# Causal attention and a dense mixture of experts: maxima by pairs of heads, three score banks, expert outputs weighed in one pass and added by POOL

## The reference, cut to what matters

```python
def _gqa(x, wq, wk, wv, wo):             # 16 heads of 8 channels, 4 key/value heads
    ...
    attn = jnp.einsum('bqhd,bkhd->bhqk', q, k) * scale
    attn = jnp.where(causal, attn, -jnp.inf)
    attn = jax.nn.softmax(attn, axis=-1)
    out = jnp.einsum('bhqk,bkhd->bqhd', attn, v).reshape(B, S, C)
    return out @ wo.T

def _moe(x, gate_w, expert_w):           # 8 experts, the best 2 weigh
    ...
    for e in range(N_EXPERTS):
        out = out + comb[:, e, None] * (t @ expert_w[e].T)
    return out.reshape(B, S, C)

h = x + _gqa(_rmsnorm(x, attn_norm_w), wq, wk, wv, wo)
out = h + _moe(_rmsnorm(h, ffn_norm_w), gate_w, expert_w)
```

## Time and profile before

| what | value |
|---|---|
| three runs | 1682.2, 1681.0, 1675.95 us; median 1681.0 |
| the profiled execution's own time | 1679.97 us |
| its span, first to last instruction | 1678.4 us |
| mean granted clock of PE, share of full speed | 0.869 |
| first blocks, up to the first piece | 887.7 us |
| 96 pieces of unit 0, guard and its DMAs | 887.7 to 946.8 us |
| the 192 steps | 946.8 to 1626 us |
| what is left of `post_h` | 1626 to 1678.4 us |

### The profile page before, as it was taken

How to read it: one execution, slowest core, us unless ns; L and a number is a source line. 1 busy time by engine, 2 the same in 40 slices (tenths; PEclk the granted TensorE clock), 3 DMA queues, 4 the chain that set the end, 5 groups by cost and what they waited for, 6 DMA issues and landing times.

```text
span 1678.4 us, 19240 instructions
## 1 busy us (share of the span) xinstructions
PE 1266.5 (75%) x6144; PEld 578.6 (34%) x6144; DVE 1185.9 (71%) x2767; ACT 719.3 (43%) x1560; POOL 515.5 (31%) x650
## 2 busy tenths in 40 slices
PE   3513988788888677565759687988899889988783
PEld 1201445454444323232323232433333333333232
DVE  4889747555555599998969685868876887688234
ACT  2434672144444410122130266546465546644751
POOL 4414770022111258767660122112111202120211
PEclk9755997999999878787765699989999999999996
DMA  3000100000000000011115201112020202000010
GB/s 96 0 0 1 47 23 1 26 1 1 0 1 0 1 10 0 1 31 21 42 24 81 30 1 28 29 17 31 2 32 7 41 1 33 4 1 1 3 39 12
DMA packets 23441, 30.14 MB, mean 18 GB/s; under 512 B 2927, under 2 KB 16111, under 8 KB 23055
## 3 DMA queue, kind: packets, MB, share of 16 engines
q1 hardware_dynamic: 20750, 26.99, 8.6%
q10 hardware_dynamic: 2592, 1.93, 0.4%
HBM read 22.50 MB, written 6.42 MB: 17 GB/s over the span
## 4 chain that ended last, share of the span: by engine, by line
PE 41%; DVE 34%; POOL 9%; ACT 8%; issue 7%; DMA 1%; ACTq 0%; DVEq 0%; POOLq 0%
PE PS L583 8%; PE PS L566 7%; DVE SS L1090 6%; PE PS L540 5%; DVE XA L1169 5%; PE PS L361 3%; DVE RB L1007 3%; PE PS L364 3%; DVE RB L1008 3%; ACT RB L1457 3%; DVE st L671 3%; POOL rs L1524 2%; PE PS L377 2%; PE PS L254 2%; PE PS L626 2%
## 5 line engine op out<-in xcount | busy, mean ns | idle before, releaser
L1457 ACT ACTIVATE RB<-PS 128x512 f32<-128x512 f32 (+3 forms) x768 | 340.3, 494 | 312.6 <-PE PS L566 308.3
L1090 DVE TENSOR_REDUCE SS<-PS 128x1 f32<-128x512 f32 (+3 forms) x768 | 374.5, 548 | 73.8 <-PE PS L543 61.9
L540 PE MATMUL PS<-B 96*128 96x512 bf16 (+3 forms) x768 | 259.3, 355 | 48.8 <-DVE XA L1169 20.7
L566 PE MATMUL PS<-B 96*128 96x512 bf16 (+3 forms) x768 | 241.7, 339 | 39.9 <-ACT RB L1457 34.7
L1658 POOL TENSOR_SCALAR_AFFINE_SELECT RB<-RB 128x512 f32<-128x512 f32 x128 | 81.3, 635 | 526.8 <-ACT RB L1457 526.6
L583 PE MATMUL PS<-RB,B 128*32 128x512 f32 (+3 forms) x1536 | 172.7, 522 | 7.6 <-ACT RB L1464 7.3
L1522 POOL TENSOR_SCALAR rs<-mv 128x4 f32<-128x4 f32 (+1 forms) x68 | 23.4, 345 | 419.0 <-DVE mv L675 417.4
L566 PEld LDWEIGHTS PS<-B 96*128 96x128 bf16 x768 | 73.2, 100 | 164.7 <-ACT RB L1457 130.8
L540 PEld LDWEIGHTS PS<-B 96*128 96x128 bf16 x768 | 77.1, 101 | 152.4 <-DVE SS L1090 87.5
L445 PE MATMUL PS<-RB,w_hspread 128*128 128x512 f32 x128 | 82.8, 784 | 61.0 <-POOL RB L1622 51.2
L935 DVE TENSOR_TENSOR RB<-RB,PS 128x512 f32<-128x512 f32 x64 | 43.8, 685 | 106.7 <-ACT RB L1336 60.5
(11 more groups left out here) (231 smaller groups left out, 2033.6 us busy)
## 6 DMA issues: line engine op xcount, KB each, us to landing
B<-scrQ SPq DMA_DIRECT2D x72, 128.0 KB
scrQ<-B SPq DMA_DIRECT2D x6, 384.0 KB, 2.6
B<-scrK SPq DMA_DIRECT2D x36, 64.0 KB
X<-in_x SPq DMA_DIRECT2D x8, 256.0 KB, 8.5
out_dram<-X SPq DMA_DIRECT2D x8, 256.0 KB, 4.1
B<-in_w SPq DMA_DIRECT2D x3, 576.0 KB, 4.7
B<-in_zeros SPq DMA_DIRECT2D x9, 128.0 KB
B<-in_rope SPq DMA_DIRECT2D x1, 1024.0 KB, 4.8
```

The source lines that it names most:

```text
L540: ins = pe.matmul(p[:, 0:w], qs[u % 3][:, h, 128 * i:128 * i + 128], keys_of(u, h)[:, 512 * c:512 * c + w], start=True, stop=not diagonal)
L566: pe.matmul(p[:, 0:w], keys_of(u, 4 * kl + z)[:, 128 * kt:128 * kt + 128], qs[u % 3][:, 4 * kl + z, 512 * qc + off:512 * qc + 512], start= ...
L1090: dve.tensor_reduce(MX[:, u % 2, i, h, c:c + 1], bank(bank_of["first", u, n])[:, 0:first_width(i, c)], AX, ALU.max).then_inc(s["mx1"], 1)
L1457: act.activation(RB[:, 4 * (step % 3) + z, 0:w], bank(bank_of["score", step, z])[:, 0:w], ACT.Exp).then_inc(s["ex2"], 1)
```

## The change

1. **Maxima by pairs of heads.** `PAIRS` takes the place of `FIRST`: PE writes the same piece for heads h and h + 1 into two neighbouring banks, and one `tensor_reduce` takes both, with two maxima as its result: 48 pairs per unit in place of 96 pieces. PE's matmuls are the same.
2. **Banks.** Scores go round banks 0, 1, 2 in all steps; pairs go round (3, 4) and (5, 6); the product has bank 7. The heads, the guard and the slices of `post_h` and of the late pass take a place in the pair ring, or in the score ring (slices 0 and 6).
3. **Spread by content.** `AHEAD` gives each step as many pairs as its share of the exponentials (weights by width, in `held`): 3 or 2 in a 512-wide step, 1 in a narrow one. A unit's pairs begin right behind those of the unit before and end at step 16 of the unit before it is used (18 for unit 1). The guard of unit u is at step 17 (19).
4. **Order.** DVE reduces one pair (or none, where two or more places of the pair ring were taken at the end of the step before), then does the slices of the *previous* step, then reduces the rest; the guard follows the last pair. ACT and POOL, too, do the slices of a step one step later, ACT between exponentials 1 and 2.
5. **Experts.** For 128 tokens PE writes all 8 experts' outputs into one pair of banks; one DVE `tensor_tensor` multiplies the 1024 columns by the weights, spread over each expert's 128 columns, into an SBUF buffer (`SHARE`, two of them, in the free tiles HN and WX). POOL adds 512 + 512, 256 + 256, 128 + 128 columns, and the last 128 to XA. DVE waits for POOL (`xs_h`) before it writes a buffer again and before the statistics (now slice 14). `post_h` has 18 slices.

```diff
-        FIRST = [(h, i, c) for h in range(8) for i in range(8) for c in range(i // 4 + 1)]
+        PAIRS = [(h, i, c) for h in range(0, 8, 2) for i in range(8) for c in range(i // 4 + 1)]
...
+            held.append(held[-1] + {512: 1920, 384: 1490, 256: 1030, 128: 760}[second_span(n, kt)[1]])
+        AHEAD = {}
+        since, GUARD_AT = 0, {}
+        for u in range(1, 8):
+            until = held[24 * (u - 1) + (19 if u == 1 else 17)]
+            for j in range(48):
+                at = next(t for t in range(192) if held[t + 1] >= since + (until - since) * (j + 1) / 48)
+                AHEAD.setdefault(at, []).append((u, j))
+            since, GUARD_AT[at + 1] = until, u
...
-        POST_SLICES = 17
+        POST_SLICES = 18
...
+        SHARE = [HN[:, :, :].rearrange("p a t -> p (a t)"), WX[:, :]]
...
-            def next_1(step):
-                ring_1[0] += 1
-                return 2 + ring_1[0] % 4 if step < 168 else ring_1[0] % 6
...
+            def next_score():
+                score_ring[0] += 1
+                return score_ring[0] % 3
+
+            def next_pair():
+                pair_ring[0] += 1
+                return 3 + 2 * (pair_ring[0] % 2)
...
+            def first_1(u, n):
+                h, i, c = PAIRS[n]
+                k = next_pair()
                 w = first_width(i, c)
                 diagonal = c == i // 4
...
+                for a in range(2):
+                    p = room(k + a)
+                    ins = pe.matmul(p[:, 0:w], qs[u % 3][:, h + a, 128 * i:128 * i + 128],
+                                    keys_of(u, h)[:, 512 * c:512 * c + w], start=True, stop=not diagonal)
+                    if diagonal:
+                        ins = pe.matmul(p[:, w - 128:w], identb[:, :], msk[:, 0, :], start=False, stop=True)
+                    banks.lend(k + a, s["mx1"], 48 * u + n + 1)
...
-                k = (4 * step + z) % 2 if step < 168 else next_1(step)
+                k = next_score()
...
-                ahead = [n for n in range(5 * r, min(5 * r + 5, 96))] if u < 7 else []
+                ahead = AHEAD.get(step, [])
                 for z in range(4):
-                    for n in ahead[z:z + 1]:
-                        first_1(step, u + 1, n)
+                    for v, n in ahead[z * len(ahead) // 4:(z + 1) * len(ahead) // 4]:
+                        if n == 0:
+                            ready_1(v)
+                        first_1(v, n)
...
             def highest(u, n):
-                h, i, c = FIRST[n]
-                dve.wait_ge(s["mm1"], 96 * u + n + 1)
-                dve.tensor_reduce(MX[:, u % 2, i, h, c:c + 1], bank(bank_of["first", u, n])[:, 0:first_width(i, c)],
-                                  AX, ALU.max).then_inc(s["mx1"], 1)
+                h, i, c = PAIRS[n]
+                w = first_width(i, c)
+                p = bank(bank_of["first", u, n], 2).rearrange("p (a t) -> p a t", a=2)
+                dve.wait_ge(s["mm1"], 48 * u + n + 1)
+                dve.tensor_reduce(MX[:, u % 2, i, h:h + 2, c], p[:, :, 0:w], AX, ALU.max).then_inc(s["mx1"], 1)
...
-                    for half in range(2):
-                        dve.wait_ge(s["mo_h"], 8 * g + 2 * j + half + 1)
-                        for q in range(4):
-                            ins = dve.scalar_tensor_tensor(XA[:, 4 * g + j, :], quarter(bank(bank_of["post", g, k, half]), q),
-                                                           comb[:, j, 4 * half + q:4 * half + q + 1], XA[:, 4 * g + j, :],
-                                                           ALU.mult, ALU.add)
...
+                    p = bank(bank_of["post", g, k], 2).rearrange("p (e c) -> p e c", e=8)
+                    dve.wait_ge(s["mo_h"], 4 * g + j + 1)
+                    if 4 * g + j >= 2:
+                        dve.wait_ge(s["xs_h"], 4 * g + j - 1)
+                    dve.tensor_tensor(SHARE[j % 2].rearrange("p (e c) -> p e c", e=8), p,
+                                      comb[:, j, :].unsqueeze(2).to_broadcast([128, 8, 128]), ALU.mult).then_inc(s["mx_h"], 1)
-                if k == 13:
+                if k == 14:
+                    dve.wait_ge(s["xs_h"], 4 * g + 4)
                     stats(g, xa_tile, "i")
...
+            for step in range(LAST_STEPS + 1):
+                ahead = AHEAD.get(step, [])
+                early = 1 if lent_last.get(step - 1, 0) < 2 else 0
+                for u, n in ahead[:early]:
+                    highest(u, n)
+                    if n == 47:
+                        guard(u)
+                if step:
+                    slices(step - 1)
+                for u, n in ahead[early:]:
...
+                if 10 <= k < 14:
+                    j = k - 10
+                    z = SHARE[j % 2]
+                    pool.wait_ge(s["mx_h"], 4 * g + j + 1)
+                    for w in (512, 256, 128):
+                        own.done(pool.tensor_tensor(z[:, 0:w], z[:, 0:w], z[:, w:2 * w], ALU.add))
+                        own.wait()
+                    pool.tensor_tensor(XA[:, 4 * g + j, :], XA[:, 4 * g + j, :], z[:, 0:128], ALU.add).then_inc(s["xs_h"], 1)
```

More of the change, by code:

```diff
@@ L54 @@
 mm1 mx1 nm1 gt1 mf1 sm1 gd1 sc2 ex2 mk2 pv2 os2 ot2 at2
[L55 removed]
+tp_h y_h po_h xo_h th_h hb_h lg_h lc_h lx_h ee_h mo_h mx_h xs_h
 """.split()
@@ L635, in tensor_program @@
             ready_1(0)
-            for n in range(96):
-                first_1(0, 0, n)
+            for n in range(48):
+                first_1(0, n)
             guard_1(0)
@@ L1191, in vector_program, with slices @@
+            def slices(step):
+                if 0 <= step - PLAG - 1 < 192:
+                    n, kt = STEPS[step - PLAG - 1]
                     if kt == 4 * GROUPS[n][2] + 3:
                         divide(n)
-                for n in ahead[2:]:
-                    highest(u + 1, n)
-                if u < 7 and r == 19:
-                    guard(u + 1)
-                if u < 7 and r == 20:
-                    guard_row(u + 1)
+                if step in GUARD_AT:
+                    guard_row(GUARD_AT[step])
@@ L1202, in vector_program @@
                     post_h(g, k)
+            for n in range(48):
+                highest(0, n)
+            guard(0)
+            guard_row(0)
+            for step in range(LAST_STEPS + 1):
[8 more added lines that the diff above has]
+                for u, n in ahead[early:]:
+                    highest(u, n)
+                    if n == 47:
+                        guard(u)
         def scalar_program():
@@ L1463, in sums @@
                     act.wait_ge(s["ot2"], n - 1)
-                act.activation(row(12 + n % 2), bank(6), ACT.Copy).then_inc(s["os2"], 1)
+                act.activation(row(12 + n % 2), bank(7), ACT.Copy).then_inc(s["os2"], 1)
             def post_h(g, k):
@@ L1496, in scalar_program @@
             act.wait_ge(s["nm_c"], 36)
-            for step in range(LAST_STEPS):
+            for step in range(LAST_STEPS + 1):
                 if step < 192:
```

126 lines of the change are left out of this document (59 added, 67 removed).

## The result

The kernel after the change takes 1768.03 us (median of four runs, 1767.02 to 1769.46), the kernel before 1678.47 beside it (four runs, 1674.99 to 1682.2): a ratio of 1.0534, 95% interval 1.0505 to 1.0563. Forecast were 1631, range 1588 to 1670. The profiled execution, one of the four, has a span of 1767.3 us against 1678.4.

| stretch, us | before | after |
|---|---|---|
| first maxima, first reduction to last | 44.7 | 53.7 |
| from there to the first exponential | 13.3 | 8.9 |
| the steps | 680.0 | 756.8 |
| tail | 51.6 | 55.8 |

The account below looks back on a forecast made before the run. No engine was full; PE, nearest to it, and ACT were taken to wait for each other in turn. Terms 0 - 30 - 10 + 1 - 27 + 18 - 2 = -50 us took the median 1681 to 1631 us, range 1588 to 1670.

Parts of the forecast that it names:

- 6 us late, three times: Statistics of chunks g = 0, 2, 4 wait for POOL's sums behind selects in diagonal steps: +18 us, bounds 0 and +36.
- The third: Rival: POOL's sums, waiting for selects in a loop, become the bound in the steps: slower, 1701 us, chance 0.08.
- The floor: In the steps: 679.2 us less 142 of PE's waits leaves about 537 us of work PE keeps.
- Pairs: Maxima by pairs save DVE 25 us over all, mostly off the path: 0, bounds -3 and +3.
- The named sign, PE's waits for reductions above 35 us: Sign that would show the forecast wrong: whole pairs make PE wait over 35 us for reductions.
- the forecast 0 (bounds -3 and +3): Prologue: pairs could gain or lose 3 us at half clock, and an earlier guard would wait longer for the DMA queue.
- Three banks, -30: In the steps: PE three scores ahead cuts its 80 us of waiting for ACT: -30 us, bounds 0 and -80.
- +1 for unit 7: Unit 7: its scores have three banks in place of six: +1 us, bounds 0 to +4.
- Spread, -10: In the steps: pieces following ACT's share take 10 of 35 us of PE's waits for maxima, bounds -30 and +10.
- Experts, -27 and +18: In the steps: PE's waits for experts' sums on DVE go, -27 us; POOL's late sums add +18.
- Tail, -2: Tail: reciprocal earlier by 3.7 us, last chunk 1.1 longer: -2 us taken, bounds -6 and +2.
- ACT idle as long as before: Sign that would show the forecast wrong: ACT's idle time does not fall.

Follow-up runs that it names:

- e1: Kernel before with the experts' part alone: products on DVE in single banks, sums on POOL, statistics one slice later; 1661.43 us, ratio 0.989.
- e8: Kernel after with slices back at the end of their own step on DVE, ACT and POOL, and DVE's division ahead of the pairs; 1663.31 us, ratio 0.9882.
- e5: e1 with pieces also spread by content: single pieces in four banks, guard at step 17, two score banks; 1642.84 us, ratio 0.9786.
- e7: Kernel after with single pieces in four places, slices back in their own step on all three engines, division ahead of the pieces; 1625.28 us, ratio 0.9669.
- g1: Kernel before with only the slices moved a step later on DVE, ACT and POOL, no experts' sums on POOL; 1776.65 us, ratio 1.0584.
- g3: e7 with two score banks in place of three, and five places for the rest; 1657.53 us, ratio 0.9875.
- g2: e7 with the first sum of 512 columns on DVE for the two chunks in the tail only; 1618.39 us, ratio 0.9629.
- f4: e7 with the first sum of 512 columns on DVE in all chunks; 1627.75 us, ratio 0.9703.
- e3: Kernel before with three score banks and three single piece banks in place of two and four, up to step 168; 1690.30 us, ratio 1.0072.

## Why the prediction was wrong

The sign, by one step: **the order of the slices**. The prediction spoke of moved slices only where it came to POOL's select, as 6 us late, three times, and gave the move itself no term in the sum. It measured 58.0 us on e1, 93.7 on the kernel before, 105.7 on the kernel after (half of it DVE's, 49.6). With it undone (e8) the kernel takes 1663.31 us, in the range, though that is 15 us under the kernel before where 50 were forecast: the pairs took the rest. The parts, each added to the one above it:

| added | steps, us | median, us |
|---|---|---|
| experts (before to e1) | -20.5 | -17.0 |
| spread (e1 to e5) | -18.3 | -18.6 |
| third score bank, heads and guard in the ring, division first, pieces placed anew between the scores (e5 to e7) | -23.1 | -17.6 |
| pairs (e7 to e8) | +33.0 | +38.0 |
| order (e8 to after) | +105.7 | +104.7 |
| together | +76.8 | +89.6 |

The rows for it stood there: the earlier trace rows have PE waiting for both pieces and experts' sums, in one ring of banks, so the question was in which order DVE would take what PE had written, and the answer could be read from the code. None of the rivals had it either. The third made the right sign (1701) of another mechanism: in the kernel after POOL is 25% busy in the steps (190.9 of 756.8), DVE waits for it for 7.5 us there, and the same sums in e8 cost nothing of the kind.

**The floor**, 537 us that PE keeps because no matmul is dropped, was wrong too as a way to count: PE's busy time in the steps went from 556.5 us (e7) to 639.4 (g1) for the same work, where the forecast moved waits alone.

**Pairs**: taken as hidden, their blocking inside bounds of -30 to +10 on all waits for maxima. They cost 33.0 us in the steps with the order right (618.1 to 651.1), 35.1 on the kernel before, 20.1 under the wrong order. Of the 25 us that DVE was to save, the page shows 17.2 (374.5 to 357.3 busy), and they bought nothing, as DVE was not the fullest engine in any unit shown; the price was what comes with pairs, two places in place of four among it. In e8 DVE waits 85.8 us for PE ahead of a reduction, in e7 45.4, and PE waits 30.4 us with the array idle for reductions, in e7 21.2. The named sign, PE's waits for reductions above 35 us, gave no clear answer: 27.7 us with the array idle, 44.2 from the weight load. By the rule of the Trainium skill that was cited there (VectorE: DVE Perf Modes, "The TRN2 errata — SBUF-src ops pay a fixed extra latency per instruction") the saving would be 48 us, and it would have argued for the pairs still more; the busy time of the first maxima, added up form by form, fell from 50.9 to 45.0 us, 123 ns for each of 48 pairs, which agrees with the rule. With the overlap of one reduction and the next taken out it fell from 44.7 to 43.8.

In the prologue the forecast 0 (bounds -3 and +3) was +9.0 for the maxima and -4.4 for what follows, +4.6. At half clock (0.52) PE's filling of a pair and DVE's reducing overlap only in part; the prologue of the kernel after, waits:

```profile
PEld PS L569 <- DVE SS L1131: 30.8, 43, 1.3
PE PS L569 <- DVE SS L1131: 10.6, 22, 0.7
DVE SS L1131 <- PE PS L569: 6.4, 12, 0.8
DVE SS L1131 <- PE PS L572: 4.0, 13, 0.6
```

Both wait in turn; before, PE waited 24.1 us from the weight load and DVE never. The guard's first DMA, which had taken 5.63 us, took 1.53 as it began 9 us later, counted from the first reduction, after the loads: the DMA share is 0.54 from 935 to 940 us before, and 0.00 from 945 to 950 after. The prediction had that pairing of start and queue, with the sign turned.

**Three banks, -30, and +1 for unit 7**: -21 in units 0 to 6 (g3 to e7), +1.0 in unit 7 (56.1 to 57.1). Right in sign and too large, and right by another way than the one given, as PE did not stand still for less. **Spread, -10**: right in sign, -18.3. **Experts, -27 and +18**: -9 forecast together, -20.5 measured. Units 1 to 6, which hold the sums, gained 26.5 us, and units 0 and 7, which hold none before the last two steps, lost 6.0, at a granted clock of 0.85 and 0.86 in place of 0.89 and 0.91. In e1 DVE doesn't wait for POOL in the steps at all, so the 18 us of lateness did not come.

**Tail, -2**: it was +4.2. The reciprocal did come 1.35 us after the last heads, in place of 4.59, as forecast. What was missed is the ACT stream behind it. The timelines of the tail, kernel after:

```profile
1719.73 0.25 DVE L1171 RECIPROCAL SS<-PS 128x16 f32<-128x16 f32 x1
...
1727.85 1.65 ACT L1263 ACTIVATE RB<-XA,rs 128x128 f32<-128x128 f32 x4 [10.55 <-POOL rs L1572]
1729.40 0.57 ACT L1518 ACTIVATE SS<-PS 128x512 f32<-128x512 f32 x1
```

The copy of the heads (L1518) stands behind the normalisation of chunk g = 6, and that now waits for POOL's sums: 9.67 us from reciprocal to copy, where the kernel before took 3.80 (L1475 at 1642.42). That is +5.9; the last chunk, from the first of its matmuls to the statistics, went from 15.75 to 17.60, +1.9 where +1.1 was forecast; with the -3.2 it comes to +4.5. The rule that was cited against this part (the Trainium skill, GPSIMD Engine Reference, "4.1 Engine selection") held in the tail: g2's one sum on DVE in each slice gave 5.8 back. In the steps the same move brought nothing: f4 is 9.4 us slower than g2 by the median, 11.6 in the steps, a part of it in units without such a sum.

Of the signs named in advance: a reduction of 1024 columns near 1.2 us (1.22), the reciprocal (1.35 us behind the heads) and the fall of PE's waits for ACT by a third (40%) came true. Units 3 and 4 at 74 and 87 did not (83.9, 105.5), but with the order put back they are 72.2 and 86.9. And "ACT idle as long as before" was named as what would prove it wrong: it was idle for longer.

What stays open: how the last 19 us of the order divide among the engines; how much of the pairs' cost is the number of places; and how much of each term is the clock and how much is cause of it, since no run holds the clock.

## What to carry to other kernels

Where one engine fills a ring of banks and another empties it, write the emptying engine's stream in the order of the filling one; an item served late does not cost its own delay but stops the whole ring, and here a moved block of cheap work cost 58 to 119 us. Read every "moved" part of a change by two lists side by side, who writes place n and who frees it, before counting instructions. Merging two items into one instruction halves the places in flight in a ring of a given size; here it lost 20 to 35 us in the steps, and 9 us even in the prologue, where the merging engine had been the one that never waited. And one negative run of a part (three banks by e3) says nothing of that part until what it took away is given back.

## What was not expected of the hardware

The moved order cost twice: PE stood still for longer, and the same matmuls took longer, 33.2 us from e8 to the kernel after (granted clock over the steps 0.95 and 0.91) and 44.7 us from the kernel before to g1 (0.96 and 0.89). Four experts' matmuls took 1.98 us at full clock (1359.93 in e8, granted clock 1.00, 2.4 GHz) and 2.84 in the kernel after, where the granted clock is 0.50 (1.2 GHz) from 1433.1 to 1436.4, after PE had stood still for 2.50 us up to 1427.10 and for the 1.97 us shown above, up to 1431.89:

```profile
1434.71 2.84 PE L665 MATMUL PS<-WW,B 128*128 128x512 f32 x4
```
